# First cross-attention of a two-layer decoder: both batches of a pair side by side in the two row halves of the array, with a new order of events

## The reference

```python
q = jnp.einsum('oc,bcn->bon', Wq, x)
kv = jnp.einsum('oc,bcn->bon', Wkv, context)
k, v = jnp.split(kv, 2, axis=1)
q = jax.nn.softmax(split_heads(q), axis=-2) * scale     # 8 heads of 64, over the head's channels
k = jax.nn.softmax(split_heads(k), axis=-1)             # over the 512 positions
v = split_heads(v)
ctx = jnp.einsum('bhdn,bhen->bhde', k, v)
out = jnp.einsum('bhde,bhdn->bhen', ctx, q)
out = jnp.einsum('oc,bcn->bon', Wout, out.reshape(b, h * e, n)) + b_out[None, :, None]
mean = jnp.mean(out, axis=1, keepdims=True)
var = jnp.var(out, axis=1, keepdims=True)
return (out - mean) * jax.lax.rsqrt(var + 1e-05) * g
```

## Time and profile before

| | |
|---|---|
| median of 3 runs | 2549.03 us (2548.66 to 2549.3) |
| the profiled execution, first to last instruction | 2542.1 us |
| what lies around it, median less that span | 6.9 us |
| PE, DVE, ACT, POOL busy over the whole | 96%, 58%, 34%, 33% |
| mean granted clock of PE | 0.978 of 2.4 GHz |
| this stage, first K to last VAR | 594.94 to 928.44, 333.5 us |

### The profile page before, as it was taken

How to read it: one execution, slowest core, us unless ns; L and a number is a source line. 1 busy time by engine, 2 the same in 40 slices (tenths; PEclk the granted TensorE clock), 3 DMA queues, 4 the chain that set the end, 5 groups by cost and what they waited for, 6 DMA issues and landing times.

```text
span 2542.1 us, 37227 instructions
## 1 busy us (share of the span) xinstructions
PE 2430.4 (96%) x12402; PEld 1975.1 (78%) x12402; DVE 1486.3 (58%) x3175; ACT 872.9 (34%) x1704; POOL 848.1 (33%) x814
## 2 busy tenths in 40 slices
PE   8999999999999988998999999999899999999987
PEld 7888888886555557776888888888788888888876
DVE  4555555567777844335455555556466666665675
ACT  3233333334666752221332333333233233333330
POOL 5322232213222326334322222311454345443352
PEclk9999999998999999998999999999899999999999
DMA  4111111000000033210210111100111011101000
GB/s 142 35 42 38 40 37 41 25 18 11 15 11 17 11 116 116 81 68 24 76 31 29 43 37 43 39 27 0 59 42 33 18 41 33 37 21 33 17 30 34
DMA packets 50118, 102.34 MB, mean 40 GB/s; under 512 B 6272, under 2 KB 9856, under 8 KB 49536
## 3 DMA queue, kind: packets, MB, share of 16 engines
q1 hardware_dynamic: 50048, 101.43, 12.3%
HBM read 99.31 MB, written 2.10 MB: 40 GB/s over the span
## 4 chain that ended last, share of the span: by engine, by line
PE 68%; issue 15%; POOL 8%; DVE 6%; ACT 1%; DMA 0%; POOLq 0%; DVEq 0%; SPq 0%; ACTq 0%
PE pb L256 18%; PE pb L258 18%; PE pb L257 18%; PE pb L533 5%; POOL probs L895 3%; PE pb L571 2%; PE pb L1080 2%; PE pb L1094 2%; POOL wl L880 1%; POOL rq L909 1%; POOL wh L878 1%; PE pb L1061 1%; PE pb L1068 1%; DVE x_kmx L1238 1%; DVE x_qmx L1247 1%
## 5 line engine op out<-in xcount | busy, mean ns | idle before, releaser
L256 PE MATMUL pb<-xTh,wh 128*128 128x512 f32 x1024 | 422.5, 413 | 19.1 <-DVE vst L723 10.0
L258 PE MATMUL pb<-xTh,wl 128*128 128x512 f32 x1024 | 403.7, 394 | 0.0
L257 PE MATMUL pb<-xTl,wh 128*128 128x512 f32 x1024 | 402.0, 393 | 0.0
L256 PE MATMUL pb<-woh,oth 128*128 128x512 f32 x768 | 316.2, 412 | 1.9 <-DVE X L823 1.9
L257 PE MATMUL pb<-wol,oth 128*128 128x512 f32 x768 | 301.6, 393 | 0.0
L258 PE MATMUL pb<-woh,otl 128*128 128x512 f32 x768 | 301.3, 392 | 0.0
L878 POOL TENSOR_SCALAR wh<-raw 128x512 fp32r<-128x512 f32 x144 | 91.9, 638 | 586.2 <-PE pb L258 429.4
L895 POOL TENSOR_TENSOR probs<-sc_sb,rs 128x512 f32<-128x512 f32 x192 | 204.5, 1096 | 211.1 <-DVE rs L791 211.1
L823 DVE TENSOR_TENSOR X<-pb,X 128x512 f32<-128x512 f32 x192 | 132.6, 691 | 221.1 <-PE pb L258 221.0
L256 PEld LDWEIGHTS pb<-xTh,wh 128*128 128x128 f32 x1024 | 194.6, 190 | 55.5 <-DVE vst L723 10.5
L258 PEld LDWEIGHTS pb<-xTh,wl 128*128 128x128 f32 x1024 | 193.7, 189 | 44.0
(11 more groups left out here) (206 smaller groups left out, 4868.2 us busy)
## 6 DMA issues: line engine op xcount, KB each, us to landing
raw<-in_a_in SPq DMA_DIRECT2D x144, 256.0 KB, 2.8
raw<-in_a_out SPq DMA_DIRECT2D x96, 256.0 KB, 2.6
f_q<-in_f_q SPq DMA_DIRECT2D x21, 512.0 KB, 3.5
f_s<-in_f_s SPq DMA_DIRECT2D x21, 512.0 KB, 4.7
probs<-in_xT SPq DMA_DIRECT2D x4, 512.0 KB, 6.7
X<-in_x SPq DMA_DIRECT2D x1, 2048.0 KB, 10.4
x_craw<-in_ctx SPq DMA_DIRECT2D x8, 256.0 KB, 2.6
x_ct<-in_ctxT_pair SPq DMA_DIRECT2D x16, 128.0 KB, 2.1
```

Source lines behind the costliest of these rows:

```text
L256: nc.tensor.matmul(out, w_hi, x_hi, start=start, stop=False)
L257: nc.tensor.matmul(out, w_hi, x_lo, start=False, stop=False)
L258: return nc.tensor.matmul(out, w_lo, x_hi, start=False, stop=stop)
```

## The change

K and Q take both batches of the pair in one event, so that four events K 0 to K 3 take the place of eight, with the matmuls of the batches in turn, each batch into its own bank. `x_ek` and `x_en` get four buffers, as `x_e` has. Units are now numbered 2 * quarter + batch, so KT 0 is batch 0 and KT 1 is batch 1, and G 0 can run when seven of the eight key transposes are copied. The reciprocals of the key sums become one event KZ. The key weights are negated once in the setup, so that the minimum is the negated maximum, and the exponential takes scale -1. POOL makes x's low part for every tile. The inverse root is an event RT in the next period, and the list is new.

```diff
-            x_ek = sb("x_ek", [P, 2, 512])
+            x_ek = sb("x_ek", [P, 4, 512])
-            x_en = sb("x_en", [P, 2, 512])
+            x_en = sb("x_en", [P, 4, 512])
...
-            ev = [("QS", 7, 1), ("XL", 0, 0), ("OUT", 0, 1), ("KT", 7, 1), ("K", 0, 0), ("Q", 0, 0), ("QT", 6, 1)]
-            ev += [("K", 1, 0), ("Q", 1, 0), ("QS", 0, 0), ("KT", 0, 0), ("QT", 7, 1), ("Y", 0, 2)]
-            ev += [("K", 2, 0), ("Q", 2, 0), ("QS", 1, 0), ("KT", 1, 0), ("G", 1, 1), ("QT", 0, 0)]
-            ev += [("XN", 0, 2)]
-            ev += [("K", 3, 0), ("Q", 3, 0), ("QS", 2, 0), ("KT", 2, 0), ("QT", 1, 0), ("M", 1, 1)]
-            ev += [("K", 4, 0), ("Q", 4, 0), ("QS", 3, 0), ("OUT", 1, 1), ("XT", 0, 2), ("KT", 3, 0), ("QT", 2, 0)]
-            ev += [("OC", 0, 1), ("K", 5, 0), ("Q", 5, 0), ("QS", 4, 0), ("KT", 4, 0), ("QT", 3, 0), ("G", 0, 0)]
-            ev += [("K", 6, 0), ("Q", 6, 0), ("QS", 5, 0), ("KT", 5, 0), ("QT", 4, 0), ("M", 0, 0)]
-            ev += [("K", 7, 0), ("Q", 7, 0), ("QS", 6, 0), ("SP", 0, -1), ("KT", 6, 0), ("QT", 5, 0), ("VAR", 0, 1)]
+            ev = [("K", 0, 0), ("RT", 0, 2), ("Q", 0, 0), ("QS", 6, 1), ("QS", 7, 1)]
+            ev += [("KT", 6, 1), ("QT", 4, 1), ("KT", 7, 1), ("QT", 5, 1), ("G", 0, 1)]
+            ev += [("K", 1, 0), ("M", 0, 1), ("Q", 1, 0), ("QS", 0, 0), ("QS", 1, 0)]
+            ev += [("KT", 0, 0), ("QT", 6, 1), ("G", 1, 1), ("KT", 1, 0), ("QT", 7, 1), ("Y", 0, 2), ("XN", 0, 2)]
+            ev += [("K", 2, 0), ("M", 1, 1), ("Q", 2, 0), ("QS", 2, 0), ("QS", 3, 0)]
+            ev += [("KT", 2, 0), ("OUT", 0, 1), ("KT", 3, 0), ("XT", 0, 2), ("QT", 0, 0)]
+            ev += [("K", 3, 0), ("SP", 0, -1), ("Q", 3, 0), ("QS", 4, 0), ("QS", 5, 0), ("KZ", 0, 0)]
+            ev += [("KT", 4, 0), ("OUT", 1, 1), ("OC", 0, 1), ("QT", 1, 0), ("KT", 5, 0), ("QT", 2, 0), ("QT", 3, 0),
+                   ("VAR", 0, 1)]
...
-                        wait(pe, xs["kexp"], 8 * q + u - 1)
-                        cols = slice(s * P, (s + 1) * P)
-                        mm3(XB["k"][u % 2][:, :], (x_wh[r, 1, cols], x_wl[r, 1, cols]), (x_ch[r, :], x_cl[r, :]), True,
-                            True).then_inc(xs["k"], 1)
+                        wait(pe, xs["kexp"], 8 * q + 2 * u)
+                        cols = slice(u * P, (u + 1) * P)
+                        for w_part, c_part in ((x_wh, x_ch), (x_wh, x_cl), (x_wl, x_ch)):
+                            for b in range(2):
+                                r = slice(64 * b, 64 * b + 64)
+                                last = nc.tensor.matmul(XB["k"][b][:, :], w_part[r, 1, cols], c_part[r, :],
+                                                        start=w_part is x_wh and c_part is x_ch, stop=w_part is x_wl)
+                                if w_part is x_wl:
+                                    last.then_inc(xs["k"], 1)
...
-                        wait(pe, xs["ekt"], 8 * q + 4 * u + 4)
+                        wait(pe, xs["ekt"], 8 * q + 7 + u)
...
+                nc.scalar.activation(x_wraw[:, 1, :], x_wraw[:, 1, :], ACT.Copy, scale=-1.0).then_inc(xs["wneg"], 1)
+                act.wait_ge(xs["wneg"], 1)
...
-                        wait(act, xs["kneg"], 8 * q + u + 1)
-                        wait(act, xs["kt"], 8 * q + u - 1)
-                        wait(act, xs["krz"], 2 * (q - 1) + b + 1)
-                        nc.scalar.activation(x_ek[:, u % 2, :], XB["k"][u % 2][:, :], ACT.Exp, bias=x_knm[:, u:u + 1],
-                                             accum_out=x_kz[:, u:u + 1]).then_inc(xs["kexp"], 1)
+                        for b in range(2):
+                            v = 2 * u + b
+                            wait(act, xs["kneg"], 8 * q + v + 1)
+                            wait(act, xs["kt"], 8 * q + v - 3)
+                            wait(act, xs["krz"], q)
+                            nc.scalar.activation(x_ek[:, v % 4, :], XB["k"][b][:, :], ACT.Exp, bias=x_knm[:, v:v + 1],
+                                                 scale=-1.0, accum_out=x_kz[:, 4 * b + u:4 * b + u + 1]
+                                                 ).then_inc(xs["kexp"], 1)
...
-                    elif kind == "VAR":
+                    elif kind == "RT":
...
-                    if kind == "XL":
-                        wait(dve, xs["xhi"], q + 1)
-                        nc.vector.tensor_tensor(x_xl[:, :], xtile(q), f32(x_xh[:, :]),
-                                                ALU.subtract).then_inc(xs["xsp"], 1)
...
-                        nc.vector.tensor_reduce(x_kmx[:, u:u + 1], XB["k"][u % 2][:, :], AX_X,
-                                                ALU.max).then_inc(xs["kmax"], 1)
...
+                            nc.vector.tensor_reduce(x_knm[:, v:v + 1], XB["k"][b][:, :], AX_X,
+                                                    ALU.min).then_inc(xs["kneg"], 1)
...
                     elif kind == "SP":
                         context_low(pool, q)
+                        input_low(pool, q)
```

More of the change, by code:

```diff
@@ L1052, in run @@
                             wait(pe, xs["xsp"], q + 1)
[L1053 to L1056, removed]
+                        wait(pe, xs["qsub"], 8 * q + 2 * u)
+                        cols = slice(u * P, (u + 1) * P)
+                        for x_part, w_part in ((x_xh, x_wh), (x_xh, x_wl), (x_xl, x_wh)):
+                            for b in range(2):
+                                r = slice(64 * b, 64 * b + 64)
+                                last = nc.tensor.matmul(XB["q"][b][:, :], x_part[r, cols], w_part[r, 0, :],
+                                                        start=x_part is x_xh and w_part is x_wh, stop=x_part is x_xl)
+                                if x_part is x_xl:
+                                    last.then_inc(xs["q"], 1)
                     elif kind == "KT":
@@ L1098, in run @@
                         wait(pe, xs["osq"], q + 1)
-                        wait(pe, xt_ready, p - 1)
-                        wait(pe, xs["mr"], 2 * NT if isinstance(p, int) and p == NT else 2 * p + 1)
+                        wait(pe, xt_ready, q)
+                        wait(pe, xs["mr"], 2 * q + 2)
                         nc.tensor.matmul(XB["gm"][:, :], x_blk[:, :], x_sq[:, :], start=True,
@@ L1106, in run @@
                         wait(pe, xs["sd"], q + 1)
-                        wait(pe, xs["mr"], 2 * NT if isinstance(p, int) and p > NT else 2 * p)
+                        wait(pe, xs["mr"], 2 * NT if isinstance(p, int) and p > NT else 2 * q + 4)
                         for k in range(KT):
@@ L1114, in pe_xattn, with prepare_ffn0 @@
                 run(p, x_steps(True, True, True))
-            def prepare_ffn0(after):
+            def prepare_ffn0(after, u):
                 if after == "VAR":
@@ L1148, in run @@
                 for kind, u, age in events:
-                    b, s = u // 4, u % 4
+                    b, s = u % 2, u // 2
                     q = p - age
@@ L1203, in act_xattn, with prepare_ffn0 @@
                 run(p, x_steps(True, True, True))
-            def prepare_ffn0(after):
-                if after == "M":
+            def prepare_ffn0(after, u):
+                if after == "M" and u == 1:
                     act.wait_ge(xs["g"], 2 * NT)
```

87 lines of the change are left out of this document (42 added, 45 removed).

## The result

The changed kernel takes **2601.24 us** (median of 4 runs, 2600.36 to 2601.87). Beside it on the same chip the kernel before took 2548.85 (4 runs, 2545.36 to 2549.3): the ratio is 1.0208, 95% interval [1.0193, 1.0222]. It is slower by 52 us.

What follows compares the result with a forecast made beforehand. TensorE was taken as nearly full, but the new order makes it wait for copies and lowers its clock: -0.6, +52.8 and +5.6 us give about +58, a median of 2607 us, range 2572 to 2620.

Steps and rivals of the forecast that it cites:

- The forecast case: Attention stage: clock low after both TensorE gaps, periods of 48.5 us, median 2607 us; chance 0.53.
- (1): K and Q on TensorE: interleaved row halves run side by side, 12.7 us a period becomes 6.4, saving 6.3.
- (2): Negated key weights: one min reduce replaces reduce and sign, 1.4 us a period off VectorE.
- (3): x's low part moves to Pool: 1.27 us off VectorE, 1.45 on Pool, nothing comes back.
- (4): New list: TensorE waits for ScalarE's copies, gaps 5.9 and 3.7 us; period 43.2 against 39.2 us.
- The clock: TensorE's clock falls in both gaps, costing about 2.2 us after the first and 3.1 after the second: period 48.5.
- The sum: Stage total: first two periods -0.6 us, six full periods +52.8, tail +5.6, together +58.
- A: Rival: the clock falls only in the first gap, periods of 45.4 us, 2588 us; chance 0.22.
- B: Rival: the clock holds throughout, periods of 43.2 us, 2575 us; chance 0.08.
- C: Rival: the row halves do not overlap, 1.4 us a period more, 2618 us; chance 0.08.
- D: Rival: ScalarE reaches the copies early enough, KT 7 starts before 3, period 33 us, 2509 us; chance 0.06.
- E: Rival: gains and waits cancel within 0.2% (5 us); chance 0.03.

Runs made afterwards that it cites:

- experiment 8: The changed kernel with a new order, root first in the list, and the variance written into the output's bank: 2499.42 us, ratio 0.9809.
- experiment 3: The kernel before with only the negated key weights (one min reduce) and x's low part on Pool: 2532.15 us, ratio 0.9945.
- experiment 6: The changed kernel with batch 1 of each K and Q step waiting until batch 0 is finished: 2611.4 us, ratio 1.0252.
- experiment 9: The fast kernel with batch 1 of each K and Q step waiting for batch 0, and each Q for its K: 2578.54 us, ratio 1.0131.
- 10: The fast kernel run once more, unchanged, in five rounds: 2501.48 us, ratio 0.9837.
- the fast kernel: The changed kernel with a new order, root first, and the variance in the output's bank: 2499.42 us, run again 2501.48 us.
- experiment 1: The changed kernel with the three matmuls of batch 0 before those of batch 1 in each K and Q event: 2600.66 us, ratio 1.0208.

## Why the prediction was right

The forecast case came: slower, 2601.2 against 2607 forecast. By its steps:

- **The parts on their own engines.** The overlap (1) held: a pair of units in 1.58 where one took 1.59. In the trace TensorE's busy time fell by some 2 us a period only, since the low clock stretches it; at full clock, in experiment 8, it is 32.9 against 38.0 (forecast 31.7). Parts (2) and (3): VectorE 27.9 (forecast 28), Pool's extra split 1.28 each. Alone they are worth 7.8 us in the stage (experiment 3); the prediction has no sum for them. The step that the prediction left open, whether halves overlap, could have been settled from the trace of before. There M, in the first half, already runs beside K of batch 1, and K is no slower: from its first product to its third it takes 0.57 (888.42 to 888.99), alone 0.58 (901.23 to 901.81 in the earlier trace rows).

```profile
887.86 0.82 PE L1086 MATMUL pb<-x_u,x_gt 64*128 64x128 f32 x5
888.42 0.49 PE L256 MATMUL pb<-x_ch,x_wh 64*128 64x512 f32 x1
888.52 0.49 PE L1086 MATMUL pb<-x_u,x_gt 64*128 64x128 f32 x3
888.75 0.39 PE L257 MATMUL pb<-x_cl,x_wh 64*128 64x512 f32 x1
888.99 0.39 PE L258 MATMUL pb<-x_ch,x_wl 64*128 64x512 f32 x1
```

- **The order (4).** The mechanism was right: KT 7 9.1 after K 0 (forecast 8.5, gap 6.42 against 5.9), KT 3 behind a gap of 3.62 (3.7), VectorE idle for 10.0 before K 1 (forecast some 7; KT 7, QT 5 and G 0 at the low clock are most of the rest). The replay gave 43.2 at full clock; with the gaps filled it measured 44.5. Block by block, K 0 to K 1, K 1 to K 3, K 3 to K 0: 13.1, 19.6, 10.5 forecast; 13.7, 20.0, 10.8 measured (K at 758.16, 771.87, 791.84, next 802.66). The 1.3 too little is spread over the three blocks; no single row accounts for it.
- **The clock.** This term was mis-sized: 5.3 a period forecast, 3.4 measured (47.9 - 44.5). Between the kernel with filled gaps and the changed one the blocks differ by 2.1, 1.3 and 0.0 us (15.80, 21.25 and 10.87 in the latter). So the first gap cost what was said (2.2) and the second 1.3 instead of 3.1. Of that 3.1, KT 3, XT and QT 0 were 1.4, K 3 0.7 and OUT 1 about 1. But the clock was back at about 803.4, so K 3 and Q 3 together took 1.75 instead of 1.58 and OUT 1 lost nothing. The prediction names an early return of the clock as a way to be wrong and gives the interleaved halves as its reason; that the clock came back early is shown, that they were the reason is not.
- **The sum.** First two periods 73.8 (74.0), six periods 288.1 (291), tail 29.1 (26.2: the clock fell there as well, 0.88, and its G 0 took 5.56). Together 391.05 against the 391.5 of 333.5 + 58. Errors of +2.9 and -2.9 cancel, so the exact hit of the span is luck within some us; the median missed by 5.8 through the 6.9 carried around the span.
- **The rivals.** A and B fail at the clock: low behind both gaps, 0.89 a period. C fails at the "x2" rows; its price for the missing overlap, 1.4 a period, is near the 1.3 of experiment 6, which removes only a part of it. D fails at its own point, KT 7 before 4.5. But its number, 2509, is what the same parts reach with an order in which no copy is late (2506.9 and 2499.4). E needed the waits to be shorter.

What is left of the slowdown: 5.3 us a period of waits, 3.4 of clock, both from the list. That the overlap is a gain in the fast order is shown by 9 against 10: without it that kernel is at 2578.5. But the 77 us are not what the overlap is worth to a kernel, since 9 keeps an order made for pairs. Experiment 3 has the same small parts with units of one batch, in the order of before, and it runs at 0.9945 of before; the fast kernel is at 0.9837. So overlap, new order and VAR's bank together are worth some 1.1%, about 27 us. Whether a better order for single units would come nearer wasn't tried.

## What to carry to other kernels

Work taken from the busiest engine is worth only what the hand-written order lets through: before counting the saving, replay the new lists and ask of each step whether what it waits for can be done by then, on an in-order engine that has other things ahead of it. Merging two units into one step doubles what stands ahead of the copy that frees a single bank; a list that puts other matmuls between two users of one bank turned 2.1% lost into 1.5% gained with the same instructions, and into 1.6 to 1.9% with the variance in another bank besides. Filling a gap with useless matmuls is a cheap experiment that parts the cost of a wait from that of the clock behind it.

## What the hardware showed that I had not expected

- **Overlap without alternation.** Three products of one row half followed in the program by three of the other began in pairs, and twelve took 1.59 us (experiment 1); so did K's batch 1 with Q's batch 0 or with M (experiment 6). Only the starts in pairs give six product times for twelve products. The Trainium skill, "TensorE: Matmul & The Clock Gate", section "The mechanism", says that matmuls start and end strictly in program order; this case's trace disagrees (the fourth began with the first, at 764.92), and the time of the whole bears the trace out.
- **The clock fell without a gap.** In experiment 9 it went from 2.4 to 1.2 GHz at 774 while TensorE was busy for over 94% of the windows shown, after half-height products in series; with the same products in pairs it stayed at 1.00 for whole periods (experiment 8). In my prediction the gaps alone were to blame. The kernel before does not settle it: from 712.97 on twelve half-height products and waits of only 0.60 and 0.44 us precede its fall at 718.5. But the next period has the same products from 755.28 on with the same waits, and the clock stays at 1.00 in it:

```profile
717.39 0.66 PE L1061 MATMUL pb<-ident,x_ek 128*128 128x128 f32 x4 [0.60 <-ACT x_ek L1157]
718.49 1.07 PE L1068 MATMUL pb<-ident,x_en 128*128 128x128 f32 x4 [0.44 <-ACT x_q L1171]
...
759.70 0.66 PE L1061 MATMUL pb<-ident,x_ek 128*128 128x128 f32 x4 [0.59 <-ACT x_ek L1157]
760.79 0.63 PE L1068 MATMUL pb<-ident,x_en 128*128 128x128 f32 x4 [0.44 <-ACT x_q L1171]
```

The same work came ahead of a fall in one period and of none in the next; what decided it, the rows do not show. In experiment 9 the clock fell in every full period. That pairs help the clock beyond the time they save rests on experiments 8 and 9; it was not parted from the difference in pace between them.
